# Two attentions with a thin FFN: tiles transposed by DMA instead of TensorE, and the second half's planned clock changed

## The reference

```python
def attn_a(x):                       # first attention: scores of LN(x), width 1024
    q, k, v = x @ w_q.T, x @ w_k.T, x @ w_v.T
    s = where(causal, q @ k.T / 32, -inf)
    return softmax(s) @ v @ w_o.T

def attn_b(x):                       # second attention: 16 heads of 64
    q, k, v = x @ Wq[h], x @ Wk[h], x @ Wv[h]            # per head h
    out = softmax(where(causal, q @ k.T / 8, -inf)) @ v
    y = x + concat_heads(out) @ Wo
    return (y - mean(y)) * rsqrt(var(y) + 1e-3) * gamma + beta

def ffn(x):                          # 1024 -> 64, each of them 16 inner units, -> 1024
    s = x @ Win + bin
    g = sum_h(relu(s[..., None] * W1 + b1) * W2) + b2
    return g @ Wout + bout

x = x + attn_a(LN(x)); x = x + ffn(LN(x))
x = x + attn_b(LN(x)); x = x + ffn(LN(x))
```

## Time and profile before

| | |
|---|---|
| median of 3 runs | 2925.57 us (2921.25 to 3174.41) |
| the profiled execution | 2910.48 us |
| its span, slowest core | 2908.9 us (the cores: 2898.7 to 2908.9) |
| busy TensorE, VectorE, ScalarE | 84%, 47%, 52% of the span |
| granted TensorE clock, mean | 0.928 |
| DMA | 277 MB, mean 95 GB/s |

### The profile page before, as it was taken

One profiled execution on the slowest core, in us unless ns is written; L12 is line 12 of the kernel. 1 busy time (PEld: TensorE's weight loads), 2 busy tenths in 40 slices (PEclk: granted clock), 3 DMA queues, 4 the chain that ended last, 5 costly groups with the idle time before them and its releaser, 6 DMA issues.

```text
span 2908.9 us, 36979 instructions; the slowest of 8 cores (2898.7 to 2908.9 us)
## 1 busy us (share of the span) xinstructions
PE 2438.2 (84%) x13327; PEld 1124.0 (39%) x13546; DVE 1371.8 (47%) x2734; ACT 1502.0 (52%) x1951; POOL 330.7 (11%) x552
## 2 busy tenths in 40 slices
PE   4978889999998748777888989999999999698773
PEld 2545565566665513223333333333333333222221
DVE  3266666565554433456554554553444343222326
ACT  3222232223332202435565776778878888599650
POOL 0000000000000001322121211211110111011001
PEclk9989999999999969988998999999999999899885
DMA  9035342121111045543444333333233232212110
GB/s 295 17 80 131 92 105 66 62 85 58 51 52 37 23 123 156 147 126 119 130 126 137 111 119 124 113 104 124 88 101 130 77 106 75 93 41 71 45 45 29
DMA packets 152832, 277.18 MB, mean 95 GB/s; under 512 B 16657, under 2 KB 107793, under 8 KB 151122
## 3 DMA queue, kind: packets, MB, share of 16 engines
q1 hardware_dynamic: 140576, 248.55, 26.5%
q0 software_dynamic: 10240, 25.70, 4.0%
q10 hardware_dynamic: 1842, 0.54, 0.1%
HBM read 223.89 MB, written 67.37 MB: 100 GB/s over the span
## 4 chain that ended last, share of the span: by engine, by line
PE 62%; DVE 17%; DMA 10%; ACT 5%; issue 4%; POOL 1%; SPq 1%; ACTq 0%; DVEq 0%; POOLq 0%
PE AVB L1467 13%; PE SB L1437 9%; PE SA L766 7%; PE AV L807 6%; PE FB L1160 6%; ACT attB L1444 4%; DMA RB<-r_scr 3%; PE FA L568 3%; PE FA L583 3%; PE FB L1306 3%; DVE bnst L279 3%; PE FB L1235 3%; DMA r_scr<-DN 3%; DVE ff L371 1%; DVE lntA L302 1%
## 5 line engine op out<-in xcount | busy, mean ns | idle before, releaser
L1444 ACT ACTIVATE attB<-SB,negCB 128x1024 bf16<-128x1024 f32 (+3 forms) x1152 | 1153.4, 1062 | 429.4 <-PE SB L1437 424.7
L1467 PE MATMUL AVB<-attB,VB 128*65 128x512 bf16 (+3 forms) x2304 | 678.0, 377 | 44.3 <-DVE U L1487 27.6
L1437 PE MATMUL SB<-qrB,krB 64*128 64x512 bf16 (+3 forms) x2304 | 440.7, 377 | 35.7 <-ACT attB L1444 20.2
L775 ACT ACTIVATE attA<-SA,cst 128x256 bf16<-128x256 f32 x272 | 125.7, 466 | 399.4 <-PE SA L766 365.9
L1467 PEld LDWEIGHTS AVB<-attB,VB 128*65 128x65 bf16 x2304 | 225.0, 114 | 260.3 <-issue 140.6
L1437 PEld LDWEIGHTS SB<-qrB,krB 64*128 64x128 bf16 x2304 | 118.0, 93 | 496.6 <-issue 495.2
L1160 PE MATMUL FB<-BT,wrB 128*128 128x512 bf16 x965 | 275.6, 394 | 18.5 <-DVE kst L1132 8.3
L766 PE MATMUL SA<-qbA,XT 128*128 128x256 bf16 (+1 forms) x2176 | 276.2, 272 | 0.3
L807 PE MATMUL AV<-Va,attA 128*128 128x512 bf16 x997 | 266.0, 388 | 4.2 <-issue 1.0
L766 PEld LDWEIGHTS SA<-qbA,XT 128*128 128x128 bf16 x2176 | 210.8, 99 | 78.0 <-issue 2.7
L1456 POOL TENSOR_SCALAR_AFFINE_SELECT attB<-attB 128x256 bf16<-128x256 bf16 (+1 forms) x256 | 121.9, 480 | 974.7 <-ACT attB L1444 974.3
(11 more groups left out here) (156 smaller groups left out, 2263.1 us busy)
## 6 DMA issues: line engine op xcount, KB each, us to landing
xp<-x SPq DMA_DIRECT2D x64, 512.0 KB, 4.6
xs<-xp SPq DMA_DIRECT2D x32, 512.0 KB, 4.1
wrB<-wk_b_s SPq DMA_DIRECT2D x16, 1024.0 KB, 6.4
wrB<-wq_b_s SPq DMA_DIRECT2D x16, 1024.0 KB, 5.9
wrB<-wv_b_s SPq DMA_DIRECT2D x16, 1024.0 KB, 6.0
RB<-r_scr POOLq DMA_DIRECT2D x64, 256.0 KB, 3.6
wrB<-wo_b_s SPq DMA_DIRECT2D x16, 1024.0 KB, 5.9
xtB<-xs SPq DMA_DIRECT2D x32, 512.0 KB, 5.4
```

Of the source, the lines that this page charges most:

```text
L775: ex = E("scalar", lambda e_: e_.activation(a[:, qo:QA], bk[:, qo:QA], AF.Exp, bias=negC[:, par:par + 1]), mm, neg_ok[c], *att_free[sl])
L1437: mm = E("tensor", lambda e_, h=h: e_.matmul(bk[:, h, qo:512], kr[64 * h:64 * h + 64, s, kc * 128:(kc + 1) * 128], qr[64 * h:64 * h + 64, ...
L1444: ex = E("scalar", lambda e_: e_.activation(att[:, sl, :, qo:512], bk[:, :, qo:512], AF.Exp, bias=negC[i % 2][:, pr:pr + 1]), mm, neg_ok[i ...
L1467: mm = E("tensor", lambda e_, h=h: e_.matmul(AV[0:65, h, qo:512], VB[:, kc, 2 * pr + h, :], att[:, sl, h, qo:512], start=(n == 0), stop=(n ...
```

## The change

It does three things.

1. Tiles are transposed by a DMA that transposes (`dma_start_transpose`, on SP), from the slot of lnt straight to XT (from c = 2 on) and lnfT, and from DRAM straight to BT without a slot. TensorE's eight transposes, the bank and the copy fall away; the slot is free when the transfer has landed. 992 of 1024 transposes on TensorE go, and 124 transfers come, of which 32 take the place of plain loads.
2. In the planned order, the FFN's projection stands 5.2 planned us after the second affine, and the chain of the first half is cut together anew without the transposition pieces. BT's loads stand behind one V piece each.
3. In the second half, `exp_end` has one entry for each step instead of two slots used in turn, a constant falls from 0.15 to 0.1, and the scaling of a pair is deferred by 18.0 instead of 16.5.

```diff
+        def start(e_):
+            if turn:
+                return e_.dma_start_transpose(out=out, in_=in_)
+            return e_.dma_start(out=out, in_=in_)
...
+    def turn_tile(slot, tok, dst, *dst_free):
+
+        o = DL(0.9, dst, cx.lnt[:, slot, :], cx.trs[slot], tok, *dst_free, turn=True)
+        cx.lnt_free[slot] = o
+        return o
...
         def aff(t):
-            st[t] = affine(tiles[t], u, t, st["r"])
-            yield 0.0
-
-        def tr(t):
-            i, tok = st[t]
-            st["e", t] = yield from transpose_tile(
-                i, tok, lnfT[:, :, t * 128:(t + 1) * 128], engs[t], cx.lnf_free)
+            i, tok = affine(tiles[t], u, t, st["r"])
+            st["e", t] = turn_tile(i, tok, lnfT[:, :, t * 128:(t + 1) * 128], cx.lnf_free)
+            yield 0.0
...
         out = [(0.0, stats, 0.0), (0.0, rstd, 3.2), (0.0, lambda: aff(0), 1.0),
-               (0.0, lambda: aff(1), 0.0), (0.85, lambda: tr(0), 1.6),
-               (0.85, lambda: tr(1), 0.2), (0.98, proj, 1.8)]
+               (0.0, lambda: aff(1), 0.0), (0.98, proj, 5.2)]
...
         def load(t):
-            i, free = cx.lnt_slot()
             r0 = n * 512 + t * 128
-            st[t] = (i, DL(0.5, lnt[:, i, :], dr["b_scr"][r0:r0 + 128, :], bsem[i], free))
-            yield 0.0
...
+            tok = DL(0.5, BT[:, :, t * 128:(t + 1) * 128], dr["b_scr"][r0:r0 + 128, :],
+                     bsem[t], bt_free[t], turn=True)
...
-    exp_end, act_end = [0.0, 0.0], [0.0]
+    exp_end, act_end = {}, [0.0]
...
-        cx.tick(max(0.0, exp_end[g % 2] - cx.clock) + 0.42 * w_)
-        act_end[0] = exp_end[g % 2] = max(act_end[0], cx.clock + 0.15) + 0.19 + 0.853 * w_
+        cx.tick(max(0.0, exp_end.get(g - 2, 0.0) - cx.clock) + 0.42 * w_)
+        act_end[0] = exp_end[g] = max(act_end[0], cx.clock + 0.1) + 0.19 + 0.853 * w_
...
-        cx.tick(max(0.0, exp_end[g % 2] - cx.clock) + 0.43 * (512 - qo) / 512.0)
+        cx.tick(max(0.0, exp_end[g] - cx.clock) + 0.43 * (512 - qo) / 512.0)
...
-        cx.defer(16.5, scale)
+        cx.defer(18.0, scale)
```

64 lines of the change are left out of this document (27 added, 37 removed).

## The result

The changed kernel takes 2980.7 us (median; 2969.0 to 3080.4), the kernel before 2930.6 in the same session: a ratio of **1.0168, 95% interval [1.0106, 1.0231]**, some 49 us slower, where 67 us of gain were forecast. The long executions at the top of both ranges are a disturbance that both kernels share, and no ratio here contains them. The profiled execution has cores from 2932.8 to 2967.4 us; the page is that of core 4.

A forecast was written before the change was run, and what follows sets the result against it. TensorE, busy 84%, was taken as the bound, with both it and ScalarE stalling in the last two stages. Terms -16 - 24 + 6 + 10 - 6 - 40 + 3 gave -67 us: 2859 us median, range 2790 to 2945.

The forecast's parts named there:

- The landing: Transposing transfers of 256 KB, issue to landing: taken as 4 us, from plain transfers of 2.3 to 3.1 us.
- the issue: SP's time over issuing one transposing transfer: 0.5 to 1.5 us.
- the tail: Two FFNs in the tail and one at the first half's end, without cover: 2 us lost each, 6 us.
- the cover in the first half: Between second affine and FFN projection: 8 us of cover against a landing about 5 us later, so nothing charged.
- the prologue: Second half's start: four independent loads straight into BT need no second round, 6 us gained, bounds 0 to 10.
- The corrected clock: Second half's planner: fewer stalls in the last two stages, higher granted clock, fewer RB waits; 40 us gained, bounds 10 and 90.
- the order shows that unchanged: Ends of stages: leftover chain pieces still pressed into the last steps, so of 46.9 us waits 15.9 stay.
- 3 us for projections at stage ends that now wait on a landing: Term of the sum for FFN projections at stage ends waiting on transfers: 3 us lost.
- -16: First half: 32 tiles' transposes taken off TensorE at 0.5 us each, 16 us gained; the other 28 counted nothing.
- my own last sentence: Forecast wrong if a transfer holds SP several us, with K, Q and weight loads queued behind, or stage-end leftover grows.
- Rival 1: The transfer becomes the bound: slower than before from a landing of about 9.5 us, some 3030 at 12; chance 0.15.
- Rival 2: Gain eaten at stage ends and starts: new waits 20 us, net -10 to -30, some 2905 us; chance 0.25.

The follow-up runs named there:

- The corrected clock alone: The kernel before with only the new planned clock of the second half, no transposing transfers: 2892.8 us, 0.9882 of the kernel before.
- the first groups: Kernel before with corrected clock; only the first two-tile FFN group of stages 0 to 5 (12 of 32 tiles) by transposing transfer: 0.9812 of before.
- XT alone: Kernel before, old clock, only the first half's LN(x) tiles by transposing transfer: 1.0075 from pair 2; 1.0062 from pair 3; the latter with stores on GpSimd 1.0036.
- the kernel with plain transfers: Changed kernel with every transposing transfer made a plain one of the same bytes into the same place, transposition left out: 1.0157 of the kernel before.

## Why the prediction was wrong

**What held.** TensorE's busy time fell by 40.0 us, the very number charged, but by luck: 40 were charged for 80 tiles at 0.5 us, and 124 tiles went, so that a tile gave 0.32 us net. The landing (4 us forecast, medians 3.2 to 4.7) held, and so did the issue (1.28 us), the tail (2 us a place, measured 1.4 to 2.0), the cover in the first half (14 of 16 places), and the prologue: the first K matmul starts 23.7 us after the second half's first load (1102.61 from 1078.91) against 27.5 before (1071.14 from 1043.64), 4 us gained of 6. The corrected clock gave 35 us for 40, but its parts were off: of the last two stages only the context's wait went, the tile waits there (12.9 us among them) stayed, and 18 of the 24 us that the table shows were gained in stages 1 to 5, for which 6 us were charged.

**The step that failed** is in the part on the clock, on the stage ends: "the order shows that unchanged", and in the sum "3 us for projections at stage ends that now wait on a landing". For the last two stages the place is about unchanged, and that is the trouble: TensorE arrives there before the affines end, so there is no cover at all, and each landing stands open (5.9 us at the end of stage 6, 4.0 to 4.5 in stage 7 and the tail; from 2400 us on 62.0 us of waits where it was 38.3). For stages 3 to 5 the order did change, by 10, 15 and 21 steps. The corrected clock alone moves the projection by 6, 7 and 5 of these steps, and BT's transfers on top of it by 6, 8 and 12, while the FFN's transfers alone leave it where the clock puts it (within 3 steps): BT's transposes had been pieces that TensorE did between V's pieces and that let the chain in. In stages 1 to 5 the wait grew from 6.0 to 61.0 us and the activation's from 5.3 to 28.1. In all, 49 of the 123.0 us pass between affines and landing, 41 of them ahead of the tail, where 3 were charged. A wait is not yet time: at the end of stage 6 the wait is 5.8 us longer than before, and stage 6 is no longer than with the clock alone (277.8 and 277.3 us). In time, the experiments put 46 us on the second half's FFN inputs (by the prediction's terms -5: 12 us of transposes gained, 3 lost at stage ends and 4 in the tail), all and more of it on second groups, last stage and tail (66 us; the first groups gain 20), and 15 on BT (by its terms -8: 12 of transposes and 6 in the prologue gained, 10 lost).

**The other wrong step** is "-16" for the first half. The transposes went, but 23 us were lost, where 14 were to be gained (16, less 2 at the end of the phase). I had looked for waits of TensorE on the landing, and found them covered, rightly. What I passed over stands in my own last sentence, that other transfers queue behind a transposing one: with 2.6 us of SyncE's row for a pair, and 4 to 6 in a busy stretch, stores of lntA came late, and VectorE, which had waited at most 3.8 us for them on any core, waited up to 24.3. With XT alone about half of the loss is shown to be this. In the changed kernel VectorE waits for the load of x instead, 27.9 us on core 4 and 37.2 us in the kernel with plain transfers, and hands this on to TensorE (30.0 us for `cst`, none before). That is not SyncE's queue but the new place of T's statistics, which meets loads that were as slow before. So what failed in this term is the assumption that work taken off TensorE leaves VectorE's row as it was. TensorE's wait for the sums at the ends of iterations (50.1 us where it was 35.3) stays unexplained.

**The rivals.** Rival 1's sign came true without its mechanism (the landing is 4 us, not 9.5). Rival 2 had two of the places, stage ends and stage starts, but priced the new waits at 20 us in all; the transfers cost 84 us net of whatever the transposes gave back, and the first half, which it left out, has 23 of them. The Trainium skill's figure of 1309 ns for each 128x128 block by the DMA crossbar (VectorE: DVE Perf Modes, section "The three transpose paths") does not hold here if blocks are taken one after the other: eight blocks landed in 3.2 to 4.7 us (medians).

## What to carry to other kernels

An engine's work that is taken off its row is worth something only if what replaces it is not later: a transposing DMA of 256 KB against 0.5 us of TensorE is a round trip of 4 us, covered for tiles that lie ahead of the need (with the first groups alone 20 us were gained) and not covered for those that an engine already stands and waits for (with the other 20 tiles 66 us were lost, part of it because a slot is held longer and the next load waits for it). Before charging a wait, ask whether the engine arrives early or late there today; an existing stall of 5 us in front of the place means that cover is zero. Ask it of every engine in the row: a place that moves forward on VectorE can meet a load that was always late. And when pieces leave a planner's list, count where each remaining piece of the chain lands in every stage, not in one, and every other transfer that shares the queue.

## What the runs showed of the hardware

A transposing transfer of 256 KB (bf16, 128 rows of 1024) holds SyncE 1.23 us at least and 1.26 to 1.29 in the median; the longest, 6.8 us, stood in the prologue behind two loads of weights, of which the plain one just before had held it 5.8 us. A plain transfer into the same scattered places holds it 0.55 to 0.62 us in the median. Both land in about the same time: 3.2 and 3.4 us on lnfT in the second half, 4.7 and 4.5 on BT. With 124 of them the packets under 512 bytes went from 16657 to 147089, and the share of the main queue from 26.5% to 32.1% of sixteen engines (30.2% with the plain ones, which make as many small packets). What these packets cost is not shown.

Loads of one queue were late beside the work of another: the loads of x shown above took 13.3 and 14.2 us, against a median of 4.8, while GpSimd's queue copied weights, and those beside the same copies in the kernel before took 12.5 and 14.0 us on the same core.
